# Mixture of experts at the end of an attention block: first layer's inputs turned two tiles ahead, evictions placed first on ScalarE, splitting waited for by pairs, expert offset read one tile ahead

## The chip, the cores and the metric

The kernel runs on one core of a Trainium2 chip. The metric is the device time of one execution in microseconds. Three runs of the kernel before gave 1023.63, 1029.57 and 1030.63 us; the median, 1029.57 us, is the time that the change is held against.

## What is computed

The input is a tensor of 64 x 128 x 128 floats. A normalised copy goes through a gated attention with four heads, and the result is added to it. Then each of the 8192 rows of 128 numbers is a token of a mixture of experts with 8 experts, of which each token uses the best two:

```python
top_w, top_i = jax.lax.top_k(gate_logits, TOP_K)
top_w = jax.nn.softmax(top_w, axis=-1)
...
for e in range(E):
    h = jax.nn.gelu(xf @ W1[e] + b1[e], approximate=False)
    out = out + w_dense[:, e:e + 1] * (h @ W2[e] + b2[e])
```

Here `W1[e]` is 128 x 512 and `W2[e]` is 512 x 128. The change touches only this last part, the experts.

## The kernel before, in words

The attention stands first and is the same in both kernels. After it, GpSimd (POOL) writes each token's row (128 values, its weight, its place) to a table in DRAM that is sorted by expert, once for the best expert of every token (`routed0`) and once for the second best (`routed1`). Each of these is 64 indirect DMAs of 128 rows (`scatter_rows`, L626). A table has 39 tiles of 256 rows, each of one expert alone, so the experts work through 78 tiles: tiles 0 to 38 from the first table, tiles 39 to 77 from the second. The second table is written while the first is worked on. A list `due` in POOL's program places its 64 scatters among the sends of tiles 0 to 30: 8 ahead of the first send, the rest spread over them. POOL sends each finished tile with two indirect DMAs (`send_rows`, L634), which wait for the tile's output and for the first half of the first layer of the tile two later.

A tile goes through these operations. SyncE loads its rows into one of 8 buffers (L525), which is free again when the tile eight earlier has been sent. TensorE (PE) turns the two blocks of 128 rows into PSUM bank `A` or `B` (L1301). ScalarE (ACT) copies the bank to fp16, `fx_h` (L792), and VectorE (DVE) computes what that rounding left out, `fx_l` (L1099). The first layer is 12 matmuls of 256 columns (L1311 to L1313): four blocks of hidden units, each from three products of high and low parts, two blocks ("a pair") to each of two PSUM banks `S`. ACT applies the gelu block by block into `hf` (L801). DVE splits `hf` pair by pair into fp16 parts `hh` (L1105) and `hl` (L1107). The second layer is a matmul for the bias (L1320) and 24 matmuls of 128 columns (L1328) into PSUM bank `PT`. ACT evicts that bank with the token's weight into one of 4 output buffers `yo` (L809), and POOL sends it.

Every engine has its own order of these, written by hand in its `tile_step(s, m)`: step `s` on PE turns tile s + 1, computes the first layer of tile s and the second layer of tile s - 1. Step `s` on ACT makes `fx_h` of tile s + 1, then the four gelus of tile s, then evicts tile s - 2. Step `s` on DVE makes `fx_l` of tile s + 1 and then splits both pairs of tile s. Two hardware loops with a body of 8 steps hold most steps; a few at both ends stand outside. Each tile's expert is known only at run time. PE and ACT read the offset of its weights or bias from a small table in SBUF into a register (`expert_of`, L421) once in each step: PE between turning and first layer, ACT between `fx_h` and the gelus. PE hands the offset on to the second layer of the next step, except at the start of a loop body, where it is read again. Engines are held together by counting semaphores: PE waits for `fx_ready` in front of the first layer, for `y_ready` in front of the bias matmul (the bank of two tiles ago must be evicted), and for `hl_ready` of both pairs in front of the 24 matmuls.

Of the kernel before, what the change touches and what calls it, by code (L numbers as in the profile page):

```python
# [68 lines left out]
def build(nc, x, ln_w, ln_b, wq, wk, wv, wb, wg_w, wg_b, wrep_w, wrep_b, Wg, bg, W1, b1, W2, b2, out):  # L69
# [24 lines left out]
    with ExitStack() as ctx:  # L94
# [138 lines left out]
        fx_h = [sbm(f"fx_h{p}", [P, TILE], F16) for p in range(2)]  # L233
        fx_l = [sbm(f"fx_l{p}", [P, TILE], F16) for p in range(2)]
# [149 lines left out]
        LOOPS = (5, 45, 77)  # L384

        def tile_steps(engine, step, extra=None):
# [4 lines left out]
            assert LOOPS[2] == TILES - 1 and all((b - a) % BODY == 0 for a, b in zip(LOOPS, LOOPS[1:]))  # L391
            e = None
            for s in range(-1, LOOPS[0]):
                e = step(s, s % BODY, e)
# [11 lines left out]
        def tile_stages(s):  # L406

            if not isinstance(s, int):
                return True, True, True, True
            return s + 1 < TILES, 0 <= s < TILES, 1 <= s <= TILES, s >= 2  # L410
# [242 lines left out]
        def _(act):  # L653
# [132 lines left out]
            def tile_step(s, m, _=None):  # L786
                tokens, first, second, weighting = tile_stages(s)
                q = m % 2
                if tokens:
                    t, p = s + 1, 1 - q  # L790
                    act.wait_ge(fxT_full, t + 1)
                    nc.scalar.activation(fx_h[p][:], AB[p][:, 0:TILE], ACT.Copy).then_inc(fx_high, 1)  # L792
                if first:
                    t, p = s, q
                    e = expert_of(act, b1_at, s, HB)
                    for pair in range(2):

                        act.wait_ge(h_full, 2 * t + pair + 1)
                        for k in range(2):
                            b = 2 * pair + k  # L800
                            last = nc.scalar.activation(hf[p][:, b, :], S[2 * p + pair][:, k * TILE:(k + 1) * TILE], ACT.Gelu,  # L801
                                                        scale=inv_hscale[:, 0:1], bias=b1_flat[:, bass.ds(e + b, 1)])
                        last.then_inc(gelu_done, 1)
                if weighting:
# [6 lines left out]
                    last.then_inc(y_ready, 1)  # L811

# [5 lines left out]
        def _(dve):  # L818
# [274 lines left out]
            def tile_step(s, m, _=None):  # L1093
                tokens, first, second, weighting = tile_stages(s)
                q = m % 2
                if tokens:
                    t, p = s + 1, 1 - q
                    dve.wait_ge(fx_high, t + 1)
                    nc.vector.tensor_tensor(fx_l[p][:], AB[p][:, 0:TILE], fx_h[p][:], ALU.subtract).then_inc(fx_ready, 1)  # L1099
                if first:  # L1100
                    t, p = s, q
                    for pair in range(2):
                        b = slice(2 * pair, 2 * pair + 2)
                        dve.wait_ge(gelu_done, 2 * t + pair + 1)
                        nc.vector.tensor_scalar(hh[p][:, b, :], hf[p][:, b, :], hscale[:, 2:3], None, ALU.mult).then_inc(hh_ready, 1)  # L1105
                        dve.wait_ge(hh_ready, 2 * t + pair + 1)
                        nc.vector.scalar_tensor_tensor(hl[p][:, b, :], hf[p][:, b, :], hscale[:, 2:3], hh[p][:, b, :],  # L1107
                                                       ALU.mult, ALU.subtract).then_inc(hl_ready, 1)
# [20 lines left out]
        def _(pe):  # L1129
# [162 lines left out]
            def tile_step(s, m, e_second=None):  # L1292
                tokens, first, second, weighting = tile_stages(s)
                q = m % 2
                e_first = None
                if tokens:
                    t, p, b = s + 1, 1 - q, (m + 1) % IN_BUFS
                    pe.wait_ge(rows_loaded[b], 16 * (t // IN_BUFS + 1) if isinstance(t, int) else (t - b) * (16 // IN_BUFS) + 16)

                    for k in range(2):  # L1300
                        last = nc.tensor.transpose(AB[p][:, k * P:(k + 1) * P], rows_in[b][:, k, 0:W], identity[:])  # L1301
                    last.then_inc(fxT_full, 1)
                if first:
                    t, p = s, q
                    e_first = expert_of(pe, w_at, s, HID)
# [53 lines left out]
```

## Time and profile before

| | us |
|---|---|
| median of three executions (1023.63 to 1030.63) | 1029.57 |
| span of the profiled execution, first to last instruction | 1159.5 |
| attention, routing and first table, up to POOL's first scatter of the second table | 676.2 |
| from there to the last send of an expert's output | 450.4 |
| from there to the end (last additions and the store) | 32.8 |

The profiled execution is the one from which every row below comes. It took 1159.5 us, some 130 us more than the executions that were only timed. So the parts of the table add up to the profiled span and not to the median, and a saving that is read from rows must first be asked whether it is there in both. Rows give start and duration in us; "idle before" is the time that the engine stood still in front of an instruction, and the arrow names what ended it. "issue" is time for which the profile shows no wait. "remote" means that a semaphore's late arrival ended the wait and that no instruction's end explains it.

### The profile page before, as it was taken

The numbers are of one execution on the slowest core, as the hardware profiler recorded it, in microseconds if no ns is written. First come the engines' busy times: TensorE is split into PE (matmuls) and PEld (weight loads), VectorE is DVE, ScalarE is ACT, GpSimd is POOL, SyncE is SP. The second block draws the span as 40 slices with busy tenths as digits, with TensorE's granted clock in tenths as the row PEclk, the third lists the DMA queues.
The fourth block names the chain that finished last, engine by engine and source line by source line (L and its number), as shares of the span: only waits on it lengthen the run. The fifth ranks groups of instructions, "written<-read, shape, count | busy, mean of one in ns | idle before, by whom it ended". The sixth has DMA issues, their size and how long they took to land.

```text
span 1159.5 us, 24862 instructions
## 1 busy us (share of the span) xinstructions
PE 722.5 (62%) x7641; PEld 534.0 (46%) x7642; DVE 754.3 (65%) x2465; ACT 609.8 (53%) x1531; POOL 442.4 (38%) x492
## 2 busy tenths in 40 slices
PE   0036888888888888739400037777677777777740
PEld 0002766666676666625200025444454565666630
DVE  4796899999999999974583014344343356666643
ACT  0024888988988889716402023344443466555540
POOL 3001233434343343300068744555555444444440
PEclk9996899999989999859755557777777899999985
DMA  9735999800000000000011121211211222333219
GB/s 202 170 73 155 179 32 155 4 0 0 0 0 0 0 0 0 0 1 0 1 40 40 54 72 48 61 53 53 58 56 56 59 81 70 94 92 94 58 39 280
DMA packets 102862, 70.40 MB, mean 61 GB/s; under 512 B 52645, under 2 KB 93158, under 8 KB 99752
## 3 DMA queue, kind: packets, MB, share of 16 engines
q1 hardware_dynamic: 92392, 42.65, 23.6%
q0 software_dynamic: 9152, 18.89, 5.0%
q10 hardware_dynamic: 1280, 8.39, 3.2%
q8 instruction: 18, 0.29, 0.1%
q14 instruction: 20, 0.16, 0.1%
HBM read 36.04 MB, written 33.61 MB: 60 GB/s over the span
## 4 chain that ended last, share of the span: by engine, by line
issue 49%; PE 17%; SPq 11%; another core or an unknown queue 6%; DVE 5%; ACT 4%; DMA 4%; POOL 2%; ACTq 1%; POOLq 0%
PE PT L1328 6%; SPq L509 4%; ACT hf L801 3%; SPq L511 3%; PE S L1311 3%; PE S L1313 2%; PE S L1312 2%; POOL expert_out L634 2%; DMA xt<-in_x 2%; DMA shared<-expert_out 1%; SPq L497 1%; PE S L1148 1%; SPq L507 1%; DVE x L832 1%
## 5 line engine op out<-in xcount | busy, mean ns | idle before, releaser
L634 POOL DMA_INDIRECT expert_out<-yo,rows_all x156 | 156.7, 1004 | 213.3 <-ACT yo L809 168.3
L626 POOL DMA_INDIRECT routed<-pay,pos x128 | 131.6, 1028 | 121.4 <-DVE pay L1059 81.1
L801 ACT ACTIVATE hf<-S,b_sb,inv_hscale 128x256 f32<-128x256 f32 x312 | 153.3, 581 | 45.6 <-remote 32.7
L716 ACT ACTIVATE L<-L,lmin 128x128 f32<-128x128 f32 x512 | 159.2, 390 | 0.4
L919 DVE CUSTOM_DVE_ANT_0 L<-S,biasN,logit_scale 128x128 f32<-128x128 f32 x512 | 148.5, 346 | 2.7 <-issue 2.0
L609 POOL TENSOR_TENSOR og<-gt,on 128x256 f32<-128x256 f32 x64 | 46.5, 726 | 231.6 <-DVE on L932 231.6
L1105 DVE TENSOR_SCALAR hh<-hf,hscale 128x512 f16<-128x512 f32 x156 | 75.5, 484 | 72.3 <-ACT hf L801 72.3
L1107 DVE SCALAR_TENSOR_TENSOR hl<-hf,hscale,hh 128x512 f16<-128x512 f32 x156 | 117.3, 752 | 5.6
L1328 PE MATMUL PT<-w_h,hh 128*128 x624 | 92.5, 226 | 44.1 <-issue 22.7
L1328 PE MATMUL PT<-w_l,hh 128*128 x624 | 93.0, 228 | 24.0 <-issue 23.9
L792 ACT ACTIVATE fx_h<-B 128x256 f16<-128x256 f32 x39 | 14.9, 383 | 174.2 <-remote 153.4
L1099 DVE TENSOR_TENSOR fx_l<-B,fx_h 128x256 f16<-128x256 f32 x39 | 16.6, 424 | 137.7 <-ACT fx_h L792 73.4
L1328 PE MATMUL PT<-w_h,hl 128*128 x624 | 91.7, 226 | 20.5 <-issue 20.5
L1311 PE MATMUL S<-fx_h,w_h 128*128 128x256 f16 x312 | 96.1, 308 | 11.3 <-DVE fx_l L1099 5.1
L1312 PE MATMUL S<-fx_l,w_h 128*128 128x256 f16 x312 | 95.7, 307 | 0.0
L1313 PE MATMUL S<-fx_h,w_l 128*128 128x256 f16 x312 | 95.4, 306 | 0.0
L711 ACT ACTIVATE ph<-PT 128x512 f16<-128x512 f32 x128 | 76.0, 595 | 26.6 <-PE B L1213 14.0
L1196 PE MATMUL PT<-identity,L 128*128 128x128 f32 x512 | 84.3, 304 | 3.3 <-DVE pl L909 2.5
L909 DVE TENSOR_TENSOR pl<-PT,ph 128x512 f16<-128x512 f32 x128 | 83.0, 683 | 2.2 <-ACT ph L711 2.2
L1328 PEld LDWEIGHTS PT<-w_h,hh 128*128 128x128 f16 x624 | 47.1, 100 | 58.4 <-issue 52.4
L1196 PEld LDWEIGHTS PT<-identity,L 128*128 128x128 f32 x512 | 65.5, 157 | 8.2 <-DVE pl L909 2.9
L1211 PE MATMUL B<-vh,ph 128*128 128x33 f16 x512 | 53.7, 182 | 19.5 <-DVE pl L909 15.1
(235 smaller groups left out, 2008.3 us busy)
## 6 DMA issues: line engine op xcount, KB each, us to landing
rows_all<-routed SPq DMA_DIRECT2D x78, 132.0 KB
routed<-blank SPq DMA_DIRECT2D x2, 5031.0 KB, 36.9
shared<-expert_out SPq DMA_DIRECT2D x16, 512.0 KB, 11.4
xt<-in_x SPq DMA_DIRECT2D x8, 512.0 KB, 25.2
shared<-in_L_conv_ln_w ACTq DMA_DIRECT2D x8, 512.0 KB, 11.7
shared<-in_L_conv_ln_b ACTq DMA_DIRECT2D x8, 512.0 KB, 10.3
out<-xt SPq DMA_DIRECT2D x8, 512.0 KB, 9.5
expert_out<-yo,rows_all POOLq DMA_INDIRECT x156
```

Of the source, the lines that this page charges most:

```text
L626: pool.indirect_dma_start(routed[k], bass.IndirectOffsetOnAxis(ap=pos[k][:, i:i + 1], axis=0), pay[:, i, :], None).then_inc(scattered[k], 16)
L634: pool.indirect_dma_start(expert_out[t // SLOT_TILES], bass.IndirectOffsetOnAxis(ap=row_place[t % IN_BUFS][:, k, W + 1:W + 2], axis=0), yo ...
L716: last = nc.scalar.activation(L[p][:, h, i, :], L[p][:, h, i, :], ACT.Exp, scale=-1.0, bias=lmin[p][:, h * R + i:h * R + i + 1])
L801: last = nc.scalar.activation(hf[p][:, b, :], S[2 * p + pair][:, k * TILE:(k + 1) * TILE], ACT.Gelu, scale=inv_hscale[:, 0:1], bias=b1_fla ...
L909: nc.vector.tensor_tensor(pl[i % 2][:], PT[i % 2][:], ph[i % 2][:], ALU.subtract).then_inc(pl_ready, 1)
L919: last = nc.vector.tensor_tensor_reduce(out=L[p][:, h, i, :], in0=S[h][:, i * P:(i + 1) * P], in1=biasN[:, h, :], scale=logit_scale[:, 0:1 ...
L1107: nc.vector.scalar_tensor_tensor(hl[p][:, b, :], hf[p][:, b, :], hscale[:, 2:3], hh[p][:, b, :], ALU.mult, ALU.subtract).then_inc(hl_ready, 1)
L1196: last = nc.tensor.transpose(PT[i % 2][:, h * P:(h + 1) * P], L[p][:, h, i, :], identity[:])
L1311: nc.tensor.matmul(dst, w1_h[:, block_at], fx_h[p][:], start=True, stop=False)
L1312: nc.tensor.matmul(dst, w1_h[:, block_at], fx_l[p][:], start=False, stop=False)
L1313: last = nc.tensor.matmul(dst, w1_l[:, block_at], fx_h[p][:], start=False, stop=True)
L1328: last = nc.tensor.matmul(PT[p][:, k * P:(k + 1) * P], h_part[p][:, b, k * P:(k + 1) * P], w_part[:, block_at], start=False, stop=b == HB ...
```

## The change

- PE turns tile s + 2 in step s, not tile s + 1. `fx_h` and `fx_l` get four buffers in place of two. The two PSUM banks stay: tile s + 2 goes to the bank of tile s, so the turning now waits for `fx_ready` of tile s.
- ACT's step begins with the eviction of tile s - 2; then come two gelus of tile s, `fx_h` of tile s + 2, and the other two gelus.
- DVE splits the first pair of tile s, makes `fx_l` of tile s + 2, and splits the second pair.
- PE waits for `hl_ready` pair by pair in the second layer.
- PE reads the offset of tile s + 1 between the first layer of tile s and the second layer of tile s - 1; ACT reads it at the end of step s. At m = 7 nothing is read ahead, so that the next step reads for itself, and what the last step of a loop body has read is dropped: PE's body has 10 reads where it had 9.
- The loops run over steps 4 to 75 (before: 5 to 76).

```diff
-        LOOPS = (5, 45, 77)
+        AHEAD = 2
+        FX_BUFS = 4
+        LOOPS = (4, 44, 76)
...
@@ ScalarE
-            def tile_step(s, m, _=None):
+            def tile_step(s, m, e=None):
...
-                if tokens:
-                    t, p = s + 1, 1 - q
-                    act.wait_ge(fxT_full, t + 1)
-                    nc.scalar.activation(fx_h[p][:], AB[p][:, 0:TILE], ACT.Copy).then_inc(fx_high, 1)
-                if first:
-                    t, p = s, q
+                if first and e is None:
                     e = expert_of(act, b1_at, s, HB)
...
+                if first:
+                    gelu_pair(s, q, e, 0)
+                if tokens:
+                    t = s + AHEAD
+                    act.wait_ge(fxT_full, t + 1)
+                    nc.scalar.activation(fx_h[(m + AHEAD) % FX_BUFS][:], AB[q][:, 0:TILE], ACT.Copy).then_inc(fx_high, 1)
+                if first:
+                    gelu_pair(s, q, e, 1)
+                if m != BODY - 1 and (not isinstance(s, int) or 0 <= s + 1 < TILES):
+                    return expert_of(act, b1_at, s + 1, HB)
+                return None
...
@@ VectorE
+                if first:
+                    split_pair(s, q, 0)
                 if tokens:
-                    t, p = s + 1, 1 - q
+                    t, b = s + AHEAD, (m + AHEAD) % FX_BUFS
                     dve.wait_ge(fx_high, t + 1)
...
+                    split_pair(s, q, 1)
...
@@ TensorE
                 if tokens:
-                    t, p, b = s + 1, 1 - q, (m + 1) % IN_BUFS
+                    t, b = s + AHEAD, (m + AHEAD) % IN_BUFS
...
+                    wait(pe, fx_ready, s + 1)
...
+                e_next = None
+                if m != BODY - 1 and (not isinstance(s, int) or 0 <= s + 1 < TILES):
+                    e_next = expert_of(pe, w_at, s + 1, HID)
                 if second:
...
-                    pe.wait_ge(hl_ready, 2 * t + 2)
                     for b in range(HB):
+                        if b % 2 == 0:
+                            pe.wait_ge(hl_ready, 2 * t + b // 2 + 1)
```

On PE the read of the offset is the row TENSOR_LOAD. In the kernel before it stands inside the loop body behind the two transposes and in front of the first layer, whose first rows follow it:

```order
L1301 MATMUL A<-identity,rows_all 128x128 [waits rows_loaded0]
L1301 MATMUL A<-identity,rows_all 128x128
L421 ISA
L421 TENSOR_LOAD w_at
L421 ISA x2
L1311 ISA [waits fx_ready]
L1311 MATMUL S2<-fx_h1,w1_h 128x256
```

In the changed kernel it stands behind the last matmul of the first layer and in front of the bias matmul of the second:

```order
L1328 REGISTER_ALU
L1328 MATMUL S3<-fx_h1,w1_l 128x256
L423 ISA
L423 TENSOR_LOAD w_at
L423 ISA x2
L1338 ISA [waits y_ready]
L1338 MATMUL PT0<-b2_parts,ones_x 128x256
L1343 ISA
L1347 REGISTER_ALU [waits hl_ready]
L1347 MATMUL PT0<-w2_h,hh0 128x128 x2
```

So the same few instructions of PE's sequencer have moved from one seam between two groups of matmuls to the other.

On ACT, a stretch of the loop body before: the gelus of one tile end, then comes the eviction, the copy `fx_h` of the next tile, the read of the offset, and the next gelus.

```order
L801 ACTIVATE hf1<-S3,b1_sb,inv_hscale 128x256
L55 REGISTER_ALU
L807 REGISTER_ALU [waits y_sent3]
L809 ACTIVATE yo3<-PT1,rows_all 128x128 [waits y_full]
L809 ACTIVATE yo3<-PT1,rows_all 128x128
L791 REGISTER_ALU
L792 ACTIVATE fx_h1<-B 128x256 [waits fxT_full]
L421 ISA
L421 TENSOR_LOAD b1_at
L421 ISA x2
L798 ISA
L801 ISA [waits h_full]
```

The same stretch in the changed kernel:

```order
L423 TENSOR_LOAD b1_at
L423 ISA x2
L55 REGISTER_ALU
L798 ACTIVATE yo0<-PT0,rows_all 128x128 [waits y_full,y_sent0]
L798 ACTIVATE yo0<-PT0,rows_all 128x128
L815 ISA
L818 ISA [waits h_full]
L818 ACTIVATE hf0<-S0,b1_sb,inv_hscale 128x256
L818 ISA
L818 ACTIVATE hf0<-S0,b1_sb,inv_hscale 128x256
L805 REGISTER_ALU
L806 ACTIVATE fx_h0<-A 128x256 [waits fxT_full]
```

The eviction's neighbours in time are nearly the same, but it now belongs to the step that begins and evicts a tile that is one younger; the copy has gone from in front of the first gelu to behind the second.

## Rows read from the trace of the kernel before

**Rows 1.** The page's first line: span and instructions of the profiled execution.

```profile
span 1159.5 us, 24862 instructions
```

**Rows 2.** Windows: length, busy (x) of PE, PEld, DVE, ACT, POOL; granted clock, DMA share, GB/s.

```profile
715.00:893.00 178.00, 125.48 (x1015) 86.42 (x1014) 70.22 (x129) 71.13 (x180) 96.19 (x99) 0.75 0.20 57
929.00:1078.00 149.00, 116.70 (x1251) 89.35 (x1249) 94.92 (x174) 87.65 (x227) 65.61 (x65) 1.00 0.33 86
```

**Rows 3.** Timeline of POOL, two tiles of the first table: start, duration, operation, idle before.

```profile
756.34 0.96 POOL L634 DMA_INDIRECT expert_out<-yo,rows_all  x1 [4.34 <-ACT yo L809]
...
760.26 0.96 POOL L626 DMA_INDIRECT routed<-pay,pos  x1 [0.31 <-issue]
...
765.31 0.95 POOL L626 DMA_INDIRECT routed<-pay,pos  x1 [0.31 <-issue]
770.57 0.96 POOL L634 DMA_INDIRECT expert_out<-yo,rows_all  x1 [4.30 <-ACT yo L809]
```

**Rows 4.** Timeline of POOL, two tiles of the second table.

```profile
1022.20 0.96 POOL L634 DMA_INDIRECT expert_out<-yo,rows_all  x1 [4.20 <-ACT yo L809]
...
1026.30 0.95 POOL L634 DMA_INDIRECT expert_out<-yo,rows_all  x1 [0.30 <-issue]
1031.45 0.96 POOL L634 DMA_INDIRECT expert_out<-yo,rows_all  x1 [4.20 <-ACT yo L809]
```

**Rows 5.** Timeline of PE and ACT, one step inside the second table's tiles.

```profile
1024.46 0.39 PE L1301 MATMUL B<-identity,rows_all 128*128 128x128 f32 x2
...
1024.87 0.28 PE L1311 MATMUL S<-fx_h,w_h 128*128 128x256 f16 x1
...
1026.28 0.38 PE L1320 MATMUL PT<-b_parts,ones_x 33*128 x1
...
1026.60 0.28 PE L1328 MATMUL PT<-w_h,hh 128*128 x2
...
1027.39 0.28 PE L1328 MATMUL PT<-w_h,hl 128*128 x2
1027.90 0.27 PE L1328 MATMUL PT<-w_l,hh 128*128 x2 [0.24 <-issue]
1027.93 0.38 ACT L792 ACTIVATE fx_h<-B 128x256 f16<-128x256 f32 x1 [3.40 <-remote]
...
1028.35 0.39 PE L1301 MATMUL A<-identity,rows_all 128*128 128x128 f32 x2
```

**Rows 6.** Waits of the stretch from 960 to 1090 us (28 tiles).

```profile
ACT fx_h L792 <- remote: 47.8, 14, 3.5
...
PEld S L1311 <- issue: 13.0, 29, 0.9
```

**Rows 7.** Groups of PE from 960 to 1090 us, the first layer's first products.

```profile
L1311 PE MATMUL S<-fx_h,w_h 128*128 128x256 f16 x113 | 31.0, 275 | 6.2 <-DVE fx_l L1099 3.0 <-issue 2.4
```

**Rows 8.** Groups of the page: both halves of DVE's splitting.

```profile
L1105 DVE TENSOR_SCALAR hh<-hf,hscale 128x512 f16<-128x512 f32 x156 | 75.5, 484 | 72.3 <-ACT hf L801 72.3
L1107 DVE SCALAR_TENSOR_TENSOR hl<-hf,hscale,hh 128x512 f16<-128x512 f32 x156 | 117.3, 752 | 5.6
```

**Rows 9.** Timeline of POOL where the experts begin.

```profile
676.25 0.95 POOL L626 DMA_INDIRECT routed<-pay,pos  x1 [1.87 <-issue]
...
701.54 0.96 POOL L634 DMA_INDIRECT expert_out<-yo,rows_all  x1 [15.50 <-ACT yo L809]
```

**Rows 10.** Timeline of ACT where the experts begin.

```profile
691.67 1.02 ACT L801 ACTIVATE hf<-S,b_sb,inv_hscale 128x256 f32<-128x256 f32 x2 [6.12 <-remote]
...
697.31 0.38 ACT L792 ACTIVATE fx_h<-B 128x256 f16<-128x256 f32 x1 [2.52 <-PE B L1301]
698.69 2.06 ACT L801 ACTIVATE hf<-S,b_sb,inv_hscale 128x256 f32<-128x256 f32 x4 [0.99 <-PE S L1313]
700.64 0.62 ACT L809 ACTIVATE yo<-PT,rows_all 128x128 f32<-128x128 f32 x2
```

**Rows 11.** Timeline of POOL, the last send of all.

```profile
1125.72 0.95 POOL L634 DMA_INDIRECT expert_out<-yo,rows_all  x1 [0.31 <-issue]
```

More of the change, by code:

```diff
@@ L232, in build @@
         pos = [sbm(f"pos{k}", [P, HALF], I32) for k in range(2)]
-        fx_h = [sbm(f"fx_h{p}", [P, TILE], F16) for p in range(2)]
-        fx_l = [sbm(f"fx_l{p}", [P, TILE], F16) for p in range(2)]
+        fx_h = [sbm(f"fx_h{b}", [P, TILE], F16) for b in range(4)]
+        fx_l = [sbm(f"fx_l{b}", [P, TILE], F16) for b in range(4)]
         hh = [sbm(f"hh{p}", [P, HB, TILE], F16) for p in range(2)]
@@ L383, in build @@
         BODY = 8
-        LOOPS = (5, 45, 77)
+        AHEAD = 2
+        FX_BUFS = 4
+        LOOPS = (4, 44, 76)
         def tile_steps(engine, step, extra=None):
-            assert LOOPS[2] == TILES - 1 and all((b - a) % BODY == 0 for a, b in zip(LOOPS, LOOPS[1:]))
+            assert LOOPS[2] == TILES - AHEAD and all((b - a) % BODY == 0 for a, b in zip(LOOPS, LOOPS[1:]))
             e = None
-            for s in range(-1, LOOPS[0]):
+            for s in range(-AHEAD, LOOPS[0]):
                 e = step(s, s % BODY, e)
@@ L811, in tile_step, with gelu_pair @@
                     last.then_inc(y_ready, 1)
+                if first:
[9 more added lines that the diff above has]
+                return None
+            def gelu_pair(t, p, e, pair):
+                act.wait_ge(h_full, 2 * t + pair + 1)
+                for k in range(2):
+                    b = 2 * pair + k
+                    last = nc.scalar.activation(hf[p][:, b, :], S[2 * p + pair][:, k * TILE:(k + 1) * TILE], ACT.Gelu,
+                                                scale=inv_hscale[:, 0:1], bias=b1_flat[:, bass.ds(e + b, 1)])
+                last.then_inc(gelu_done, 1)
             act.wait_ge(table_ready, 2)
@@ L1310, in tile_step @@
                             block_at = bass.ds(e_first + (2 * pair + k) * P, P)
[L1311 to L1313 removed]
+                            nc.tensor.matmul(dst, w1_h[:, block_at], fx_h[f][:], start=True, stop=False)
+                            nc.tensor.matmul(dst, w1_h[:, block_at], fx_l[f][:], start=False, stop=False)
+                            last = nc.tensor.matmul(dst, w1_l[:, block_at], fx_h[f][:], start=False, stop=True)
                         last.then_inc(h_full, 1)
+                e_next = None
+                if m != BODY - 1 and (not isinstance(s, int) or 0 <= s + 1 < TILES):
+                    e_next = expert_of(pe, w_at, s + 1, HID)
                 if second:
@@ L1331, in tile_step @@
                     last.then_inc(y_full, 1)
-                return e_first
+                return e_first, e_next
             pe.wait_ge(table_ready, 2)
```

40 lines of the change are left out of this document (15 added, 25 removed).

## The prediction

> **What bounds the kernel now.** I read the span first [rows 1], because it decides what the other rows are worth: the profiled execution is 1159.5 us long, and the median of the timed ones is 1029.57 us. Some 130 us are in the trace and not in the time that counts. The next question is where. The windows [rows 2] show the two kinds of stretch among the experts. In neither is any engine full: POOL is busy for 96.2 of 178 us in the first, PE for 116.7 of 149 us in the second.
>
> POOL's own timeline gives the period. In the first table two tiles take 770.57 - 756.34 = 14.2 us [rows 3], in the second 1031.45 - 1022.20 = 9.25 us [rows 4]. POOL itself starts an indirect DMA every 1.26 us when it has one (760.26 to 765.31 is four of them, 5.05 us) [rows 3], and then stands for 4.2 to 4.3 us, waiting for an eviction.
>
> Who is late in the second table is seen in one step of PE [rows 5]. PE turns a tile at 1024.46 and is through at 1024.85. ACT, which waits for exactly that, starts `fx_h` at 1027.93, 3.1 us later, and its wait of 3.40 us is put down as "remote": no instruction ended there. PE went on meanwhile, paused at 1027.39 to 1027.90 and resumed just as ACT did. So PE works, but its "done" signals are held back; the release comes 0.7 us after POOL's burst of four sends ends (1026.30 + 0.95 = 1027.25) [rows 4, 5]. This occurs once in two tiles: 47.8 us in 14 waits over 28 tiles [rows 6]. In the first table, where the bursts also hold the scatters, the period is longer.
>
> Are those holds in the timed executions? Add up a run without them. POOL starts the second table's scatters at 676.25 [rows 9]. Up to the send of tile 30 it has 64 scatters and 62 sends, 126 x 1.26 = 159 us. Its idle time ahead of the first send is 15.5 us [rows 9], 6.1 of them a hold on ACT [rows 10], so 9.4 remain: 844.6. By then PE may be four tiles ahead (four output buffers), so 43 tiles of 47 are left at PE's pace. That pace, from turning to turning, is 1028.35 - 1024.46 = 3.89 us, less the pause of 0.51 - 0.11 = 0.40, so 3.49 us [rows 5]: 43 x 3.49 = 150, to 994.7. Some 3 us for the last eviction and send, and 1159.5 - (1125.72 + 0.95) = 32.8 us behind it [rows 1, 11], make 1030.5 us. The median is 1029.57. I therefore take the timed executions as nearly free of holds: **bound by POOL up to tile 30 and by PE from then on**. That is the choice on which the forecast rests.
>
> **The change part by part.** All terms are for such a run; what they would be in the profiled one stands behind.
>
> Turning two tiles ahead takes away any wait for `fx_l` in front of the first layer. In the trace PE idles there 6.2 us in 28 tiles, 0.22 us each: 3.0 us for DVE, 2.4 for "issue" [rows 7]. In the first table POOL hides it. In the 43 tiles at PE's pace it can bring 43 x 0.22 = 9.5 us at most, and nothing at least, since part of it is the waiting that holds cause. I take half, -4.7 us. The turning now waits for `fx_ready` of tile s; behind it the 12 matmuls of the same tile are queued, which needed the same signal, so the wait is not new for them. It also needs its rows a tile earlier: eight input buffers cover that.
>
> The read of the offset on PE moves from the seam behind the transposes to the seam behind the first layer. No row shows the read itself. PE's weight loader idles 13.0 / 29 = 0.45 us in front of the first layer [rows 6], while PE idles 0.22 us there [rows 7]: half of it is covered by matmuls already in PE's queue. At the new seam, the bias matmul starts 1.41 us behind the first layer's first matmul, where 12 at 0.11 us would take 1.32, so 0.1 us is open now [rows 5]. The move then costs between 0 and 0.45 us a tile, 0 to 19 us in 43 tiles. Nearest to it is the old seam, so I take 0.06 us, +2.6 us. The tenth read per body of eight tiles costs at most 0.45 / 8 us a tile, 2.4 us; I take +1.0.
>
> The Trainium skill ("DMA: Bandwidth & Descriptors", Latency and other measured facts) gives such a register load a floor of about 600 ns. With none of it covered the move would cost an estimated 0.6 x 43 = 26 us by that page; no row here shows it open for that long.
>
> The eviction first on ACT: ACT's work is 2.06 for four gelus, 0.62 for the eviction, 0.38 for the copy [rows 10], 3.1 us a tile, under PE's 3.49. No reordering of it sets the pace while PE is full. `yo` now waits for the output buffer (the send of four tiles ago) in front of the gelus, and behind it stand both gelus and the next `fx_h`, for which PE waits a tile and more later. In the first table that wait is real, but POOL then has three or four tiles queued, some 14 us of work, and cannot run dry through it. It gains once, at the start: the first eviction stood behind four gelus (698.69 to 700.64) [rows 10] on the way to POOL's first send. POOL also waits for the first pair of tile 2's first layer, which is what those gelus waited for. So it gains up to 1.95 us; I take -1.7. A send in every tile starts some 2 us earlier, with no effect on POOL's total.
>
> Splitting waited for by pairs: the split of a pair takes 0.48 + 0.75 = 1.24 us [rows 8]. From the end of a first layer, ACT and DVE need about 1.35 + 1.24 us (the second pair's gelus with what is left of the first's, then its split) to the last `hl`; PE turns, computes a first layer and a second one in between, 3.49 us. The old wait is covered by 0.9 us in every tile but the last, where nothing stands between: there the new one saves half a second layer, 0.7 us. I take -0.7.
>
> Sum: -4.7 + 2.6 + 1.0 - 1.7 - 0.7 = -3.5 us, so **1026 us**, from -14 (everything at its best) to +20 (the read open throughout).
>
> In the profiled execution more must happen. ACT's 3.1 us of work between release and burst (fx_h, four gelus) leave the path of the eviction, which is now first, so the 9.25 us can fall to the 5.05 of POOL's burst + 0.7 + 0.62 + about 0.6 = 7.0. The profiled span may drop by tens of us with the timed runs hardly moving.
>
> **The rivals.** *The holds are in the timed runs too.* For it: the rows tie them to POOL's bursts, not to the profiler. Against it: the sum above leaves them no room, and 130 us must be somewhere. The Trainium skill ("NOTIFIC — the notification-queue block", Constraints, capacities, measured rates) says that emitting the trace's records costs the engine zero cycles. By that, the profiler can't be the cause, and the holds should be there always; the gap between 1159.5 and 1029.57 us speaks against it. What it would give, from rows: at most (9.25 - 7.0) / 2 = 1.1 us in each of 43 tiles, 48 us, so 981; half of that if half of the holds are real, **1005 us**.
>
> *The read of the offset becomes the bound.* Slower. If PE's sequencer has no lead left behind the first layer (its matmuls are fed as fast as they run), the read stands open in each tile, from the point at which the queue holds less work than the read takes. Price: 0.45 - 0.06 = 0.39 us x 43 = +17 us, the tenth read +1.4 more, so 1026 + 18 = **1044 us**. For it: 0.1 us is already open at that seam [rows 5]. Against it: at the old seam more than half was covered.
>
> *The read-ahead does not do what it says:* at m = 7 and at a body's end nothing is gained. It then costs the +1.0 counted, and leaves 1027 us.
>
> **How the numbers follow.** A measurement of this kernel can tell about 1% from no change, 10.3 us: 1019.3 to 1039.9. The forecast's case (with the last rival) has 0.53 and its own range is 1018 to 1036. The holds' case has 0.30, nearly all of it below 1019. The read's case has 0.12, and 0.05 goes to starvation through the eviction's new wait, near 1045; about all of these 0.17 is above 1040. So faster 0.31, same 0.52, slower 0.17. To leave out no more than 2 in 10, the range reaches to 998 (two thirds of the holds' case and more is then inside) and to 1044.
>
> **What would show it.** In the trace of the changed kernel: idle time in front of the first layer's matmuls near zero, and idle in front of the bias matmul not over 0.2 us a tile (right), or 0.4 us and more (the read's case). POOL's period in the second table at 7 to 8 us for two tiles in place of 9.25. POOL still the fuller engine in the first table. The forecast is wrong if the timed runs fall with the profiled span (then holds were real), or if POOL's first-table pace in the timed runs is not 1.26 us an operation, so that slack was hidden in my sum.

## The result and the profile after

The changed kernel took 1036.93 us, the median of 20 executions (1027.82 to 1040.62), against 1028.89 us for the kernel before, also of 20 (1021.63 to 1030.78). The ratio is 1.0066 (95% interval 1.0049 to 1.0083). 1026 us was forecast: the change costs 8 us where it was to gain 3.5. The time lies in the stated range, but the sign is wrong and the interval excludes no change, and that is what has to be explained.

The page's head for the changed kernel:

```profile
span 1033.6 us, 25026 instructions
...
PE 669.7 (65%) x7641; PEld 519.1 (50%) x7642; DVE 754.3 (73%) x2465; ACT 616.3 (60%) x1531; POOL 454.6 (44%) x492
```

The profiled execution's own time is 1035.35 us, its span plus 1.8. The 1159.5 us of [rows 1] have shrunk by 126 us, and the timed runs rose by 8. No wait of this trace is put down as "remote" where [rows 6] had 47.8 us of them. Of the kernel before two more traces were taken (first and second control below): spans 1033.2 and 1025.9 us, and no "remote" either. So the holds belonged to one execution of the kernel before, not to the kernel, and the comparison from here on is with these two controls.

Windows of the changed kernel, then of the second control (columns as in [rows 2]):

```profile
715.00:850.00 135.00, 98.59 (x1054) 79.04 (x1054) 76.08 (x137) 77.45 (x194) 103.61 (x104) 0.97 0.27 78
850.00:975.00 125.00, 119.25 (x1400) 101.26 (x1401) 104.54 (x192) 100.15 (x249) 83.11 (x75) 1.00 0.44 114
```

```profile
715.00:850.00 135.00, 103.20 (x1075) 79.06 (x1072) 77.78 (x139) 78.15 (x195) 103.31 (x105) 0.97 0.28 79
850.00:975.00 125.00, 122.30 (x1434) 103.09 (x1435) 107.77 (x197) 103.74 (x258) 74.23 (x76) 1.00 0.43 114
```

In the 125 us of the second window PE does 1400 instructions in place of 1434, and POOL is busy 83.11 us for 75 operations where it was 74.23 for 76. POOL in the changed kernel at the end of the second table's scatters (answers to [rows 3]):

```profile
841.76 0.96 POOL L636 DMA_INDIRECT expert_out<-yo,rows_all  x1 [0.30 <-issue]
843.02 0.95 POOL L628 DMA_INDIRECT routed<-pay,pos  x1 [0.30 <-issue]
844.28 0.96 POOL L628 DMA_INDIRECT routed<-pay,pos  x1 [0.30 <-issue]
845.55 1.01 POOL L636 DMA_INDIRECT expert_out<-yo,rows_all  x1 [0.30 <-issue]
```

It never waits longer than 0.31 us from its first send to the last scatter, and starts an operation each 1.26 us or, where one lasts longer, somewhat later: in the mean each 1.32 us here and 1.30 us in the controls. The 4.3 us of waiting in [rows 3] are gone, in both kernels. This is what the prediction took for the timed runs: POOL sets the pace to the last scatter, PE from there on.

The start of the experts, answers to [rows 9] and [rows 10], first POOL, then ACT:

```profile
676.59 0.96 POOL L628 DMA_INDIRECT routed<-pay,pos  x1 [1.87 <-DVE pay L1100]
...
690.50 1.03 POOL L636 DMA_INDIRECT expert_out<-yo,rows_all  x1 [4.08 <-PE S L1328]
```

```profile
687.29 1.07 ACT L818 ACTIVATE hf<-S,b_sb,inv_hscale 128x256 f32<-128x256 f32 x2
688.89 0.62 ACT L798 ACTIVATE yo<-PT,rows_all 128x128 f32<-128x128 f32 x2 [0.54 <-PE PT L1347]
689.88 1.02 ACT L818 ACTIVATE hf<-S,b_sb,inv_hscale 128x256 f32<-128x256 f32 x2 [0.36 <-PE S L1328]
```

The eviction now waits for PE's matmul (0.54 us), not behind four gelus, and the first send starts 13.9 us after the first scatter.

Where an execution reaches the experts differs by itself: the first scatter of the second table starts at 676.6 us and, in a second trace, 676.3 us with the change, at 680.0 and 673.1 without. So the experts' own stretch is cut at events that every trace has. In us, two traces of each kernel, first trace / second trace:

| from | to | before | after | mean change |
|---|---|---|---|---|
| first scatter of second table | first send | 15.4 / 15.5 | 13.9 / 14.0 | -1.5 |
| first send | last scatter | 152.4 / 151.8 | 153.8 / 154.4 | +2.0 |
| last scatter | bias matmul of tile 36 | 5.1 / 4.8 | 9.1 / 9.3 | **+4.3** |
| tile 36 | bias matmul of tile 72 | 124.3 / 124.4 | 125.6 / 125.5 | +1.2 |
| tile 72 | bias matmul of tile 77 | 15.2 / 15.2 | 15.5 / 15.5 | +0.3 |
| tile 77 | end of last send | 8.1 / 8.1 | 6.5 / 6.5 | -1.6 |
| whole stretch | | 320.5 / 319.8 | 324.4 / 325.3 | **+4.7** |

Tile 36 means the bias matmul of its second layer, the sign that PE has got as far. One line makes most of the loss: where the kernel goes over from POOL's pace to PE's, PE is a tile further back. The rest of this text is mostly about that line.

The table's line overstates that loss, since it ends inside the handover. Once PE sets the pace, two bias matmuls stand 3.29 us apart inside a loop body, in both kernels. From tile 36 to tile 37 it is 3.29 us with the change, but 4.5 and 4.7 us in the controls, which stand still for rows once more there. Counted to tile 37 the loss at the handover is **3.0 us** (12.37 and 12.64 us behind the last scatter, against 9.55 and 9.50), and from tile 37 to tile 72 it is 2.5 us (122.3 us twice, against 119.8 and 119.7). The +4.3 and +1.2 of the table are the same 5.5 us, parted a tile earlier.

### The profile page after: what moved, and what is told of

Its sections match the earlier page's. It is cut to its first block, busy times and chain, and to the rows that moved or that the text cites. A ratio compares the mean times of both kernels' runs of the same rounds, so it can differ in the third digit from the quotient of the medians.

```text
span 1033.6 us, 25026 instructions
## 1 busy us (share of the span) xinstructions
PE 669.7 (65%) x7641; PEld 519.1 (50%) x7642; DVE 754.3 (73%) x2465; ACT 616.3 (60%) x1531; POOL 454.6 (44%) x492
## 4 chain that ended last, share of the span: by engine, by line
PE 31%; DVE 28%; issue 15%; POOL 12%; DMA 9%; ACT 3%; SPq 1%; DVEq 0%; POOLq 0%; ACTq 0%
POOL routed L628 9%; PE PT L1347 7%; DVE L L928 6%; DVE pl L918 4%; PE S L1326 3%; PE S L1328 3%; PE S L1327 3%; POOL expert_out L636 2%; DMA expert_out<-yo,rows_all 2%; DMA rows_all<-routed 2%; DMA xt<-in_x 2%; DVE rowstat L446 2%; DVE xt L953 2%; PE PT L1338 2%; DMA shared<-expert_out 2%
## 5 line engine op out<-in xcount | busy, mean ns | idle before, releaser
L636 POOL DMA_INDIRECT expert_out<-yo,rows_all x156 | 167.5, 1074 | 75.0 <-PE S L1328 39.4
L818 ACT ACTIVATE hf<-S,b_sb,inv_hscale 128x256 f32<-128x256 f32 x312 | 159.3, 568 | 58.0 <-PE S L1328 57.9
L1326 PE MATMUL S<-fx_h,w_h 128*128 128x256 f16 x312 | 86.5, 277 | 3.7 <-issue 3.0
L1347 PE MATMUL PT<-w_h,hh 128*128 x624 | 87.6, 223 | 0.6 <-DVE hl L1120 0.6
L1347 PE MATMUL PT<-w_l,hh 128*128 x624 | 86.6, 221 | 0.0
L1328 PE MATMUL S<-fx_h,w_l 128*128 128x256 f16 x312 | 86.6, 278 | 0.0
L1327 PE MATMUL S<-fx_l,w_h 128*128 128x256 f16 x312 | 86.5, 277 | 0.0
L1315 PE MATMUL A<-identity,rows_all 128*128 128x128 f32 x78 | 16.2, 291 | 89.1 <-DMA rows_all<-routed 87.9
L798 ACT ACTIVATE yo<-PT,rows_all 128x128 f32<-128x128 f32 x156 | 48.7, 363 | 35.5 <-PE PT L1347 35.3
L1209 PEld LDWEIGHTS PT<-identity,L 128*128 128x128 f32 x512 | 64.8, 156 | 10.1 <-DVE pl L918 2.9
L1224 PEld LDWEIGHTS B<-vh,ph 128*128 128x128 f16 x512 | 43.4, 99 | 39.4 <-issue 32.3
```

The lines of the kernel that those rows point to most:

```text
L636: pool.indirect_dma_start(expert_out[t // SLOT_TILES], bass.IndirectOffsetOnAxis(ap=row_place[t % IN_BUFS][:, k, W + 1:W + 2], axis=0), yo ...
L1209: last = nc.tensor.transpose(PT[i % 2][:, h * P:(h + 1) * P], L[p][:, h, i, :], identity[:])
L1326: nc.tensor.matmul(dst, w1_h[:, block_at], fx_h[f][:], start=True, stop=False)
L1327: nc.tensor.matmul(dst, w1_h[:, block_at], fx_l[f][:], start=False, stop=False)
L1328: last = nc.tensor.matmul(dst, w1_l[:, block_at], fx_h[f][:], start=False, stop=True)
L1347: last = nc.tensor.matmul(PT[p][:, k * P:(k + 1) * P], h_part[p][:, b, k * P:(k + 1) * P], w_part[:, block_at], start=False, stop=b == HB ...
```

## The experiments

Each kernel was run beside the kernel before on the same chip. Where a quoted expectation gives theories letters, C is the lead: that PE can be one tile less ahead of POOL. None of the kernels leaves out or changes a part of the computation.

**Control: the kernel before, unchanged, for a trace without the holds.**

> The kernel before, unchanged, for a trace of it that can be laid beside that of the changed kernel. Theory A (PE's seams: the reads of the offset between the two layers, three of them at a body's start, cost PE time in the second table): PE's period in the second table is shorter here than the changed kernel's 3.45 us a tile, about 3.3, and POOL's pace in the first table is the same as there, 1.31 us an operation. Theory B (POOL: its indirect DMAs last longer beside the new order on ACT and DVE): POOL's pace here is 1.26 to 1.27 us an operation, and PE's period about the same 3.45 us. If the holds are an accident of one execution, the span is near 1028 us; if they come with every trace of this kernel, near 1160 us.

Measured: 1034.97 us in its one execution (before: 1028.91), span 1033.2. The trace has no "remote" wait; it is the first "before" of the table. Its time is 6 us above the median of the timed runs and not 130, so the holds' rival falls: the timed runs did not have them. Both theories of the expectation have a small part of the truth: PE's period from tile 36 to 72 is 3.45 us against 3.49, POOL's operations 1.30 us apart against 1.32. The large line of the table is in neither.

**PE's read put back in front of the first layer, all else as changed.**

```diff
-                if m != BODY - 1 and (not isinstance(s, int) or 0 <= s + 1 < TILES):
-                    e_next = expert_of(pe, w_at, s + 1, HID)
```

> The changed kernel, but PE reads the offset where it did before, in front of the first layer. Theory A: 5 to 8 us faster than the changed kernel, 1029 to 1032 us, and the idle time of 1.2 us in front of the bias matmul once in eight tiles is gone. Theory B: unchanged, 1035 to 1038 us.

Measured: 1030.99 us (12 executions), ratio to before 1.0026 (0.9995 to 1.0057). That is what theory A expected: the moved read costs some 6 us of the 8, 1036.93 - 1030.99. In the trace the stretch is 323.4 us, only 1.5 under the changed kernel's mean. Tile 36 to 72 takes 123.0 us: 2.6 less than with the moved read, 1.3 less than before the change. Those 1.3 us lie between tiles 36 and 37 alone: from tile 37 to 72 it takes 119.7 us, just what the controls take. And the last scatter is still followed by tile 36 only after 9.5 us and by tile 37 after 12.8: the loss at the handover has nothing to do with the read.

Waits of PE from 860 to 970 us (33 tiles), of the changed kernel and of the second control:

```profile
PE PT L1338 <- issue: 4.8, 4, 1.3
...
PEld PT L1338 <- issue: 12.3, 32, 1.5
PEld S L1326 <- issue: 1.6, 4, 0.7
```

```profile
PE PT L1320 <- issue: 1.6, 4, 0.5
PE S L1311 <- issue: 0.9, 3, 0.4
...
PEld PT L1320 <- issue: 8.6, 32, 0.8
PEld S L1311 <- issue: 3.0, 8, 0.6
```

The idle time in front of the bias matmul rose, and on the matmul side (PE) it is in 4 places only, one in each pass of the loop body. There the timeline of the changed kernel reads:

```profile
932.97 0.27 PE L1328 MATMUL S<-fx_h,w_l 128*128 128x256 f16 x1
934.45 0.38 PE L1338 MATMUL PT<-b_parts,ones_x 33*128 x1 [1.21 <-issue]
...
937.53 0.27 PE L1328 MATMUL S<-fx_h,w_l 128*128 128x256 f16 x1
937.74 0.38 PE L1338 MATMUL PT<-b_parts,ones_x 33*128 x1
```

The first pair is the body's first step. It makes three reads, its own offset in front of the first layer, and at this seam the next step's and the second layer's: 1.21 us stand open. In the next step the same seam has no wait at all, read included. So within a body the read is hidden; at its start it is not. The distances of the bias matmuls say the same: of the 2.6 us, 2.1 lie in the two steps at the start of each of the four bodies between tiles 37 and 72.

**No read-ahead in the first step of a body and in the step before it** (and the step m = 7 now reads ahead, so 9 reads in a body).

```diff
-                if m != BODY - 1 and (not isinstance(s, int) or 0 <= s + 1 < TILES):
+                if m not in (LOOPS[0] - 1, LOOPS[0]) and (not isinstance(s, int) or 0 <= s + 1 < TILES):
```

> The changed kernel, but PE does not read ahead in the first step of a loop body, so that two reads never stand one behind the other between the layers. Theory A: about 0.6 us less at each body's start in the second table, five of them, so 2 to 4 us faster than the changed kernel, 1033 to 1035 us. Rival (all reads between the layers cost the same): under 1 us.

Measured: 1033.22 us (8 executions), 1.0074 (1.0039 to 1.0110). Tile 36 to 72: 124.4 in place of 125.6 us, as the reading says. But the whole stretch, 325.1 us, is no shorter, and against its own runs of the kernel before the ratio is not below the changed kernel's 1.0066. The 2 to 4 us that were expected did not come: inconclusive.

**The changed kernel, turning one tile ahead again; reads, evictions and waits as changed.**

```diff
-        AHEAD = 2
+        AHEAD = 1
...
-        LOOPS = (4, 44, 76)
+        LOOPS = (5, 45, 77)
```

> The changed kernel with the turning back at one tile ahead; eviction first, order on DVE, waits by pairs and reads ahead stay. Theory C: the lead comes back, 4 to 6 us faster than the changed kernel, 1031 to 1033 us; the last scatter to the bias matmul of tile 36 is back at 5 us. Rival D: as the changed kernel, within 1.5 us.

Measured: 1050.51 us (6 executions), 1.0230 (1.0187 to 1.0273), not faster but 14 us slower than the changed kernel. After the last scatter tile 36 follows in 5.6 us and tile 37 in 9.9: the lead is back, as expected. But tile 36 to 72 takes 141.7 us. Its waits from 860 to 980 us:

```profile
PEld PT L1338 <- issue: 18.0, 31, 1.5
...
PE PT L1338 <- issue: 10.0, 24, 1.2
PEld S L1326 <- issue: 9.5, 23, 0.8
PE S L1326 <- DVE fx_l L1110: 2.1, 7, 0.4
```

Here the read does stand open, in 24 places, 0.42 us in the mean, and PE waits for `fx_l` as well. This is the slower rival of the prediction with its price or a little more (0.39 us a tile forecast, 1044 us). Turning two ahead is what hides it, since this kernel and the changed one differ in nothing else but the loops' bounds. How it does so is my reading, which no run takes apart: the turning and a first layer of a tile whose inputs are long there keep PE's queue full.

**The kernel before with turning two ahead alone** (`AHEAD = 2`, four `fx` buffers, the wait of the turning for `fx_ready` of tile s, steps 4 to 75; reads, eviction and waits as before).

> The kernel before with the turning two tiles ahead as its only change (reads, eviction, order of DVE and one wait for the splitting as before). Theory A: no slower than before, 1024 to 1030 us, since the reads stand where they did. Theory B: if it is the turning ahead that lengthens POOL's operations, 1034 us and more.

Measured: 1039.35 us (6 executions), 1.0108 (1.0079 to 1.0138). Last scatter to tile 36 is 9.3 us and to tile 37 12.6, as in the changed kernel; and then PE waits for rows, so that tile 37 to 72 takes 128.6 us:

```profile
PE B L1313 <- DMA rows_all<-routed: 4.5, 4, 2.5
```

So the part that was to gain 4.7 us loses 10 when alone. Theory A is out. Theory B has the time but not the reason: POOL's sends are 1.01 us long here, hardly more than the controls' 0.99.

**The kernel before, whose rows are loaded one send later.** Turning, reads and evictions are untouched; it is as if there were seven input buffers.

```diff
+            ROWS_HELD = 7
...
-                wait(sp, y_sent[t % YO_BUFS], sent_count(t % YO_BUFS, t - IN_BUFS))
+                wait(sp, y_sent[(t - ROWS_HELD) % YO_BUFS], sent_count((t - ROWS_HELD) % YO_BUFS, t - ROWS_HELD))
```

> The kernel before, but SyncE loads a tile's rows only when the tile seven earlier has been sent, where it was eight: PE's possible lead over POOL is one tile shorter, as it is when the turning stands a tile further ahead. Theory C (the lead: turning two ahead costs what one input buffer less would): 4 to 10 us slower than before, the time from the last scatter to the bias matmul of tile 36 grows from 5.1 us to about 9, as in the changed kernel (9.1 us), and PE waits for rows at loop bodies' starts. Rival D (the lead does not matter, the other order of instructions does): no slower than before, within 1.5 us.

Measured: 1038.42 us (6 executions), 1.0134 (1.0089 to 1.0179). Last scatter to tile 36: 9.9 us, to tile 37: 13.4. With nothing but the rows changed, one tile of lead less brings the loss at the handover, 3.9 us by tile 37 where the change has 3.0 (and late rows in the PE-bound part besides):

```profile
PEld B L1303 <- DMA rows_all<-routed: 3.6, 4, 1.4
PE B L1303 <- DMA rows_all<-routed: 2.9, 4, 1.2
```

**More lead: 16 input buffers for the changed kernel, 16 input and 8 output buffers for the kernel before**, both with a body of 16 steps. The buffers lie over tensors that are dead by then, so the additions of the first table's outputs were cut into smaller pieces.

```diff
-    IN_BUFS = 8
+    IN_BUFS = 16
...
-        BODY = 8
+        BODY = 16
```

> The changed kernel with 16 input buffers instead of 8 (and so a loop body of 16 steps; output and fx buffers lie on memory of the routing that is dead by then). Theory C: the lead of PE over POOL is no longer cut by the turning two ahead, so the last scatter to the bias matmul of tile 36 falls from 9 us to 5 or less; with half as many loop starts it is 5 to 9 us faster than the changed kernel, 1028 to 1032 us. Rival D (lead does not matter): that distance stays at 9 us, and only the loop starts bring 2 to 4 us.

> The kernel before with 16 input and 8 output buffers and a body of 16 steps, everything else as before. Theory C: PE can be up to three tiles further ahead when POOL has written the second table, so the bias matmul of tile 36 comes before the last scatter, and the kernel is 7 to 12 us faster than before, 1016 to 1022 us. Rival D: within 4 us of before, from the loop starts alone.

Measured: 1034.78 us (12 executions), 1.0064 (1.0037 to 1.0092) for the changed kernel, 1029.18 us, 0.9992 (0.9967 to 1.0017) for the kernel before. Hardly any gain from the one, none from the other, and neither is what theory C expected: I had thought the buffers were the only limit. Behind the last scatter tile 36 follows in 7.8 us in the changed kernel (5 or less was expected). In the kernel before it comes 18.8 us ahead of that scatter, as expected, and still nothing is gained. The traces say what else is a limit. First the changed kernel with 16 buffers, then the kernel before with 16 and 8, at the last scatter (844.3 and 843.4 us):

```profile
848.93 0.68 PE L1315 MATMUL B<-identity,rows_all 128*128 128x128 f32 x2 [4.79 <-DMA rows_all<-routed]
```

```profile
847.86 0.69 PE L1313 MATMUL B<-identity,rows_all 128*128 128x128 f32 x2 [21.47 <-DMA rows_all<-routed]
```

Both rows are the turning of tile 39, the first of the second table. Its rows can't be loaded before the last scatter has landed, and both kernels turn it 4.5 to 4.6 us after that scatter starts. In the kernel before PE had run so far ahead that it stood 21.47 us for it. Lead that ends at that door is worth nothing. With 8 buffers tile 39 is turned 7.4 us after the last scatter in the changed kernel and 7.2 in the second control, so more buffers can give 2.7 us at most. By tile 37 only part of that is left: 12.3 us behind the last scatter in the changed kernel (12.4 and 12.6 with 8 buffers), 8.1 in the kernel before (9.6 and 9.5). While PE stood at the door its granted clock fell, and what it does next runs at the lower of TensorE's two levels, 1.2 GHz in place of 2.4. The windows from 848 to 852 us (columns as in [rows 2]), the two kernels with more buffers, then the second control:

```profile
848.00:852.00 4.00, 3.07 (x14) 2.08 (x14) 0.23 (x1) 1.60 (x5) 3.08 (x4) 0.50 0.94 246
```

```profile
848.00:852.00 4.00, 3.77 (x16) 2.11 (x17) 0.96 (x3) 1.74 (x4) 3.09 (x4) 0.50 0.93 255
```

```profile
848.00:852.00 4.00, 3.56 (x42) 3.07 (x43) 1.93 (x4) 2.87 (x8) 2.98 (x3) 1.00 0.39 103
```

The kernel before with more buffers then loses more than the 1.5 us that it has gained: tile 37 to 72 takes 123.0 us in place of 119.7. Why isn't known.

**Eviction behind the gelus, all else as changed.**

```diff
-                if weighting:
-                    t, p, b = s - 2, q, (m - 2) % YO_BUFS
...
-                    last.then_inc(y_ready, 1)
                 if first:
                     gelu_pair(s, q, e, 0)
...
                 if first:
                     gelu_pair(s, q, e, 1)
+                if weighting:
+                    t, p, b = s - 2, q, (m - 2) % YO_BUFS
...
+                    last.then_inc(y_ready, 1)
```

> The changed kernel with ACT's eviction behind the gelus again. Theory A: as the changed kernel, within 2 us. Theory B in the form that the eviction's place makes ACT and POOL collide: faster by up to 7 us, with POOL's sends in the first table back at 1.0 us from the changed kernel's 1.07.

Measured: 1043.28 us (6 executions), 1.0150 (1.0100 to 1.0200). It is neither as fast as the changed kernel (theory A) nor faster (theory B): the eviction's place is worth about 6 us in the changed kernel. In the trace the first send comes 16.5 us after the scatter (13.9 with it first), the end takes 8.1 us (6.5). From 860 to 980 us POOL waits for evictions, and ACT, behind its own eviction, for PE:

```profile
POOL expert_out L636 <- ACT yo L806: 43.5, 34, 2.9
ACT hf L818 <- PE S L1328: 28.8, 34, 2.4
```

**The kernel before with the eviction first, and nothing else.**

> The kernel before with one part of the change alone: ACT's eviction ahead of the copy and the gelus. Turning one tile ahead, reads and waits as before. From the traces: POOL's first send 1.5 us earlier and its last one 1.5 us earlier relative to PE; so 2 to 4 us faster than before, 1025 to 1027 us. Theory C says that nothing here shortens the lead: the last scatter to the bias matmul of tile 36 stays at 5 us.

Measured: 1030.24 us (12 executions), 1.0046 (1.0013 to 1.0080). The start falls to 13.5 us and the end to 6.4, 3.6 us together, tile 36 stays at 4.9 us as expected, and still the kernel isn't 2 to 4 us faster; by the interval it is a little slower. First send to last scatter takes 154.0 us in place of 152.1, tile 36 to 72 126.5 in place of 124.4. The whole stretch is 320.5 us, that of the kernel before (320.5 and 319.8). POOL's groups from 680 to 850 us show where the first of these comes from; the changed kernel, then the second control:

```profile
L636 POOL DMA_INDIRECT expert_out<-yo,rows_all x66 | 68.0, 1031 | 23.9 <-issue 19.5 <-PE S L1328 4.1 <-ACT yo L798 0.3
```

```profile
L634 POOL DMA_INDIRECT expert_out<-yo,rows_all x69 | 68.5, 993 | 26.4 <-issue 14.6 <-ACT yo L809 9.7 <-PE S L1313 2.1
```

and of the kernel with only the eviction moved:

```profile
L636 POOL DMA_INDIRECT expert_out<-yo,rows_all x70 | 72.5, 1035 | 24.5 <-issue 19.2 <-PE S L1326 5.3
```

A send takes 1.03 us in the mean in place of 0.99. It isn't every send that is a little longer: most take 0.96, some 1.20, as here, with DVE's `hh` beside it:

```profile
863.75 1.20 POOL L636 DMA_INDIRECT expert_out<-yo,rows_all  x1 [0.31 <-issue]
864.03 0.48 DVE L1116 TENSOR_SCALAR hh<-hf,hscale 128x512 f16<-128x512 f32 x1
...
865.25 0.96 POOL L636 DMA_INDIRECT expert_out<-yo,rows_all  x1 [0.30 <-issue]
```

From the first send to the last scatter these kernels all have 117 operations of POOL with 35.7 us of idle time between them, so the +2.0 of the table is their length and nothing else: 62 sends of 0.04 us more make 2.6 us, and the scatters give 0.7 back. Whether `hh` is the cause isn't shown. In the controls and in this kernel each of the operations over 1.1 us has `hh` beside it (18, 14 and 22 of them), but so have a third of those under 1 us; and in the two traces of the changed kernel it is only 25 of 43. That the eviction's place sets the lengths isn't shown either: the changed kernel with the eviction behind the gelus has sends of 1.05 us there too.

**Both kernels once more.**

> The changed kernel again, for a second trace and its time on the same chip as the next one. The stretch from POOL's first scatter of the second table to its last send was 324.4 us in the first trace against 320.5 in that of the kernel before: 3.9 us, where the medians differ by 8. If one trace each was a fair sample, it is again 324 to 325 here, and the rest of the difference in time lies elsewhere; if not, this stretch differs by 6 to 8 us between this run and the next. The last scatter to the bias matmul of tile 36 again 9 us.

> The kernel before again, a second trace of it without holds, and a control on the comparison: ratio 1.000 within its interval. The last scatter to the bias matmul of tile 36 again 5 us; the whole stretch of the experts 317 to 321 us.

Measured: 1036.95 us (9 executions), 1.0089 (1.0056 to 1.0121), and 1028.29 us (12), 1.0003 (0.9974 to 1.0032). They are the second traces of the table, and agree with the first ones within 0.3 us in every part but the POOL-bound one (0.6). So 3.3 of the 8.0 us between the timed runs are not in the traced stretch (4.7). The granted clock of the whole run bears on it: over 29 executions of the changed kernel the span goes down by 5.6 us for each 0.01 of clock, over 80 of the kernel before by 7.0. The former ran at 0.874 in the mean (mean span 1034.6 us), the latter at 0.879 (1026.7). At the latter's clock the changed kernel's line gives 1032.0 us: 5.3 us above, close to the traces' 4.7. That is an estimate and takes the clock for the cause, which isn't shown: the kernel before with 16 and 8 buffers ran at 0.864 in the mean and was no slower for it. Why the changed kernel's clock was lower isn't known; in the traces it is the same for both kernels among the experts (windows above), and the attention before them is the same code.

## Why the prediction was wrong

The step that failed is the first term of the sum, turning two tiles ahead at -4.7 us. It came out at +3.0: nothing gained, and a price that the prediction put at nothing. The mechanism that I left out stands in one sentence of the prediction, where it says that PE "also needs its rows a tile earlier: eight input buffers cover that". They don't. PE may turn tile t only when tile t - 8 is sent. While POOL sets the pace, PE runs up to this limit and stands there for rows (from 715 to 850 us 27.0 us with the change, 18.4 in the second control); when POOL's scatters end, what PE has done beyond the turning is its head start for the PE-bound part. Turning one ahead it has done the first layer of tile t - 2 and is at t - 1; turning two ahead it is at t - 2. The rows of PE at that moment, changed kernel first (last scatter at 844.28), then the second control (840.35), show the same tile 38 being turned 2.2 and 2.0 us after the last scatter:

```profile
846.51 0.43 PE L1315 MATMUL A<-identity,rows_all 128*128 128x128 f32 x2 [1.54 <-DMA rows_all<-routed]
847.39 0.28 PE L1326 MATMUL S<-fx_h,w_h 128*128 128x256 f16 x1 [0.45 <-issue]
...
849.99 0.38 PE L1338 MATMUL PT<-b_parts,ones_x 33*128 x1 [1.12 <-issue]
```

```profile
842.30 0.44 PE L1301 MATMUL A<-identity,rows_all 128*128 128x128 f32 x2 [0.97 <-DMA rows_all<-routed]
843.28 0.28 PE L1311 MATMUL S<-fx_h,w_h 128*128 128x256 f16 x1 [0.55 <-issue]
...
845.15 0.38 PE L1320 MATMUL PT<-b_parts,ones_x 33*128 x1 [0.39 <-issue]
```

But the bias matmul that follows is tile 35's in the first and tile 36's in the second. One more tile of PE's work is left to do, 3.29 us, and from there PE is the bound. Not all of it is paid, because the kernel before stands for the rows of tile 39 once more and the changed one does not, again changed kernel first, the turning of tile 39 and the bias matmul of tile 37:

```profile
851.65 0.39 PE L1315 MATMUL B<-identity,rows_all 128*128 128x128 f32 x2
...
856.65 0.38 PE L1338 MATMUL PT<-b_parts,ones_x 33*128 x1
```

```profile
847.51 0.44 PE L1301 MATMUL B<-identity,rows_all 128*128 128x128 f32 x2 [0.53 <-DMA rows_all<-routed]
...
849.85 0.38 PE L1320 MATMUL PT<-b_parts,ones_x 33*128 x1
```

That makes 12.4 and 9.5 us behind the last scatter, the 3.0 us from above. Nine kernels bear it out. From the last scatter to tile 36 it is 4.8 to 5.6 us in the three that turn one ahead with 8 buffers (to tile 37: 9.5 to 9.9), 9.1 to 10.1 in the five that turn two ahead with 8 buffers (12.3 to 13.4), and 9.9 (13.4) in the kernel before when its rows come a send later.

Step by step:

- *What bounds the kernel*: right. POOL to the last scatter, PE behind it; and the fall of the profiled span with the timed runs hardly moving came as said. That its sum met the median within 1 us is partly luck: POOL's operations are 1.30 us apart and not 1.26, 5 us more over 126 of them, and its wait ahead of the first send is 5.7 us in the second control and not 9.4. PE's pace behind tile 37 is 3.42 us a tile with the starts of the bodies, where 3.49 was taken. The rival that the holds are real fell with the first control.
- *Turning two ahead, -4.7 us*: nothing gained, and its price forgotten. The 0.22 us a tile before the first layer [rows 7] was a number of the held execution: in the second control PE idles 0.9 us there over 33 tiles, 0.03 us each. The gain is read best with the read at its old place: from tile 37 to 72, 119.7 us against 119.8 and 119.7, so none. The price is the +3.0 above.
- *The moved read, +2.6, and the tenth read, +1.0*: together +3.6, and +2.6 measured between tiles 36 and 72 (125.6 against 123.0), 2.1 of it where the bodies start. Its size is about right, but not its form: the forecast spread most of it over every tile. The timed difference is larger, 6 us, between the two terms' sum and the rival's price. Without the turning two ahead the read costs 20 us (1050.51 against 1030.24, with DVE's and ACT's new order in it), so the "read becomes the bound" rival was priced well; what I hadn't seen is that the first edit pays for the second.
- *Eviction first, -1.7 at the start*: -1.5 measured. Nothing was forecast for the end: -1.6 there, since the last evictions no longer stand behind gelus. Left out: longer operations of POOL, +2.0, whose cause is open. By itself, in the kernel before, the eviction first gains nothing.
- *Waiting by pairs, -0.7*: not tried alone; no row of the table shows it apart.

With the handover counted to tile 37 the traces' sum is -1.5 + 2.0 + 3.0 + 2.5 + 0.3 - 1.6 = +4.7 where -3.5 was forecast. Of the 8.2 us between them, 7.7 are the turning two ahead: 3.0 of lost lead and the 4.7 of gain that wasn't there. The other terms missed too, by +2.0 and -1.6 above all, but nearly cancel.

Left open: the 3 us by which the timed runs differ more than the traced stretches, which go with the clock but whose cause isn't shown; and why moving the eviction alone lengthens the PE-bound part by 2.1 us. No kernel tried here beats the kernel before: the nearest are the changed kernel with PE's read at its old place (1.0026) and the kernel before with more buffers (0.9992), and neither can be told from it.

## What to carry to other kernels

A stage that runs further ahead takes its inputs earlier, and with a fixed number of buffers that comes out of the lead of everything behind it. Ask at the place where the bound passes from one engine to the other how many tiles the second has in hand, and what it waits for there: one tile less costs up to one tile at the second engine's pace (here 3.0 of 3.3 us). Before adding buffers for it look for a door that all must pass (here the second table, complete only with its last scatter): beyond it lead is worth nothing. And of a profile whose span doesn't match the timed runs take a second one before any size is read from it.

## What the runs showed of the hardware

- One execution of the kernel before took 130 us longer than its median, with ACT's wait for PE ending just behind POOL's burst and no instruction's end to explain it [rows 4, 5]; in two more traces of the same kernel and eleven of changed ones there is no such wait. What brought it about isn't known.
- A read of an offset by PE leaves no idle time in front of 28 of 32 bias matmuls of the changed kernel (860 to 970 us) and about 1.2 us in front of the other four, where three reads come close together. With turning one tile ahead it stands open 24 times from 860 to 980 us, 0.42 us in the mean.
- An indirect DMA of POOL is 0.96 us in most cases and about 1.2 in some. In the kernel before all 32 that are over 1.1 us (two traces, first send to last scatter) have DVE's `hh` beside them, with the change 25 of 43; the cause isn't shown.
- After PE had stood 4.8 and 21.5 us for rows, its granted clock was 0.50 (1.2 GHz) from 848 to 852 us, where the kernels with 8 buffers have 1.00; the bias matmul there took 0.58 us in place of 0.38.
- Over 80 executions of the kernel before, with a granted clock of 0.87 to 0.89 in the mean of the run, the span is 7.0 us shorter per 0.01 of clock (correlation -0.76); over 29 of the changed kernel 5.6 us (-0.78).
